# An attention stage of 32 samples written out in full in place of a loop on each engine

## What is computed

```python
x = x + 0.5 * ffn(layernorm(x))      # 2 of 8 experts per sample, chosen by its first row
x = x + attention(layernorm(x))      # 16 heads of 16, rotary positions, causal softmax
x = x + 0.5 * ffn(layernorm(x))

def attention(x):                    # b, t, d = 32, 512, 256
    q, k, v = split(x @ Wqkv.T)      # then heads; q and k are rotated
    scores = q @ k.T / 4, masked above the diagonal
    return merge(softmax(scores) @ v) @ Wo.T
```

## Time and profile before

| | |
|---|---|
| median of 3 runs | 2465.36 us (2464.51 to 2467.04) |
| the profiled execution | 2469.6 us |
| its span, first to last instruction | 2467.8 us |
| mean granted TensorE clock | 0.974 |
| TensorE (PE) busy | 2275.3 us, 92% of the span |
| VectorE (DVE) busy | 1969.7 us, 80% |
| ScalarE (ACT) busy | 1365.5 us, 55% |
| GpSimd (POOL) busy | 1275.4 us, 52% |

### The profile page before, as it was taken

How to read it: one execution, slowest core, us unless ns; L and a number is a source line. 1 busy time by engine, 2 the same in 40 slices (tenths; PEclk the granted TensorE clock), 3 DMA queues, 4 the chain that set the end, 5 groups by cost and what they waited for, 6 DMA issues and landing times. The chain is left out here.

```text
span 2467.8 us, 61020 instructions
## 1 busy us (share of the span) xinstructions
PE 2275.3 (92%) x18828; PEld 1422.1 (58%) x18828; DVE 1969.7 (80%) x4349; ACT 1365.5 (55%) x2567; POOL 1275.4 (52%) x1458
## 2 busy tenths in 40 slices
PE   2999999389999999999999999999999995999999
PEld 1666666146655555565555555655655552666666
DVE  4777776589889888898898898888988973777776
ACT  2455444046656666665566566656666663554454
POOL 2666665345445545554454455445544523666664
PEclk9999999589999999999999999999999997999999
DMA  4566665334543444344444444533443323566664
GB/s 159 167 210 202 196 195 181 78 61 95 97 88 87 88 88 87 88 92 84 88 87 92 83 88 92 98 82 81 95 94 88 79 53 103 188 198 195 206 207 163
DMA packets 281250, 296.35 MB, mean 120 GB/s; under 512 B 46096, under 2 KB 264048, under 8 KB 280944
## 3 DMA queue, kind: packets, MB, share of 16 engines
q1 hardware_dynamic: 280400, 291.34, 47.0%
q10 hardware_dynamic: 544, 1.05, 0.1%
HBM read 140.08 MB, written 83.89 MB: 91 GB/s over the span
## 5 line engine op out<-in xcount | busy, mean ns | idle before, releaser
L815 ACT ACTIVATE at_probs<-at_st_ps 128x512 f32<-128x512 f32 x1280 | 754.3, 603 | 553.6 <-PE at_st_ps L915 548.8
L745 DVE TENSOR_REDUCE at_mx<-at_mx_ps 128x1 f32<-128x512 f32 (+3 forms) x1408 | 842.4, 635 | 199.5 <-PE at_mx_ps L898 189.3
L667 POOL TENSOR_SCALAR_AFFINE_SELECT at_probs<-at_probs 128x512 f32<-128x512 f32 x512 | 318.7, 635 | 774.5 <-ACT at_probs L815 774.5
L896 PE MATMUL at_mx_ps<-at_k_stack,at_q_stack 128*128 128x512 f16 (+3 forms) x2048 | 539.8, 302 | 17.7 <-DMA at_k_stack<-qk_image 12.0
L915 PE MATMUL at_st_ps<-at_q_stack,at_k_stack 128*128 128x512 f16 (+3 forms) x2048 | 495.1, 303 | 43.1 <-issue 27.0
L898 PE MATMUL at_mx_ps<-mask,identb 128*128 128x128 bf16 x2048 | 387.0, 220 | 0.0
L420 ACT ACTIVATE f_h<-f_h_ps,f_b1s 128x512 f32<-128x512 f32 x256 | 175.9, 687 | 362.0 <-PE f_h_ps L462 351.0
L915 PEld LDWEIGHTS at_st_ps<-at_q_stack,at_k_stack 128*128 128x128 f16 x2048 | 167.6, 98 | 317.5 <-ACT at_probs L815 164.7
L932 PE MATMUL at_pv_ps<-at_probs,at_v 128*32 128x512 f32 (+3 forms) x4096 | 328.9, 439 | 1.2 <-POOL at_probs L667 0.6
L478 PE MATMUL f_y_ps<-f_w2hi,f_hhi 128*128 128x256 f16 x1024 | 279.3, 273 | 0.0
L478 PE MATMUL f_y_ps<-f_w2lo,f_hhi 128*128 128x256 f16 x1024 | 279.3, 273 | 0.0
(11 more groups left out here) (118 smaller groups left out, 3980.6 us busy)
## 6 DMA issues: line engine op xcount, KB each, us to landing
at_q_stack<-qk_image SPq DMA_DIRECT2D x192, 128.0 KB
at_k_stack<-qk_image SPq DMA_DIRECT2D x192, 128.0 KB, 4.4
f_x<-in_x SPq DMA_DIRECT2D x32, 512.0 KB, 5.7
f_w1hi<-w_hi SPq DMA_DIRECT2D x128, 128.0 KB, 2.5
f_w1lo<-w_lo SPq DMA_DIRECT2D x128, 128.0 KB, 2.2
f_b2s<-in_b SPq DMA_DIRECT2D x128, 128.0 KB, 3.8
f_w2hi<-w_hi SPq DMA_DIRECT2D x128, 128.0 KB, 4.2
f_w2lo<-w_lo SPq DMA_DIRECT2D x128, 128.0 KB, 4.2
```

The source lines that it names most:

```text
L667: nc.gpsimd.affine_select(out=ap, in_=ap, compare_op=ALU.is_ge, fill=0.0, base=0, pattern=[[0, d] for d in dims] + [[1, P]], channel_multi ...
L745: nc.vector.tensor_reduce(o_ap, i_ap, AX_X, ALU.max).then_inc(max_done, 1)
L815: nc.scalar.activation(probs[:, c, :], st_ps[c % 2][:], ACT.Exp, scale=DH ** -0.5).then_inc(exp_done, 1)
L896: nc.tensor.matmul(bank[:, at * w:at * w + w], q_stack[s.par][:, h, i * P:(i + 1) * P], k_stack[s.par][:, h // 2, 0:w], start=True, stop=F ...
```

## The change

`schedule` loses its hardware loop. One Python loop writes all samples from -1 to 32 out with `k = 0`. Each engine gets the same operations in the same order with the same waits; the values of the waits and the DRAM addresses of samples 3 to 28 become constants, as they were before and behind the loop. Buffers, semaphores and the other phases stay.

```diff
         def schedule(eng, slot):
             for g in (2, 3):
                 slot(At(0, -2), g)
-            for c in range(-1, 3):
-                for g in range(4):
-                    slot(At(0, c), g)
-            with eng.Fori(0, (B - 6) // 2) as k:
-                for c in (3, 4):
-                    for g in range(4):
-                        slot(At(k, c), g)
-            for c in range(B - 3, B + 1):
+            for c in range(-1, B + 1):
                 for g in range(4):
                     slot(At(0, c), g)
             slot(At(0, B + 1), 0)
```

## The result

The changed kernel takes 2428.05 us (median of 4 runs, 2427.58 to 2428.63) where the kernel before took 2464.94 us beside it: a ratio of 0.985, with a 95% interval of 0.9833 to 0.9867, or 36.9 us less. The forecast was 2429.3 us.

What follows compares the result with a forecast made beforehand. TensorE's pace bounds the attention phase, with 12 branches back stalling it. 23 us of stalls and 13 us of clock drops, 36.1 us by whole samples, off the 2465.4 us median give 2429.3 us; range 2419 to 2440 us.

Steps and rivals of the forecast that it cites:

- four branch-free samples: Steady-state attention samples without a branch back: 47.43, 47.52, 47.20 and 47.22 us, mean 47.34, taken as the straight code's pace.
- 46.99 behind a branch: Sample after a branch that left the clock alone, 46.99 us; used only for the range's end, a gain of 44.5 us.
- All alike: Sign of being right: attention samples of 47.0 to 47.5 us from store to store, all alike.
- a sign of being wrong: Samples over 47.6 us with no wait to show for it would make the four samples no fair measure.
- The two parts: Attention loop: 12 branches at 1.9 us, 23 us, plus seven pairs of samples slowed by clock drops, 13 us; together 36.
- rival 1: Clock still drops in attention, at some rate with dense work: gain only 23 us, time 2442.4 us; chance 0.07.
- Register work at nothing: Loop's register operations for waits and addresses, on all engines, are covered, so removing them gains nothing.
- More code at nothing: Writing out 26 samples instead of two costs nothing: the loop already loads its code again each iteration.
- The branch's price: TensorE's compare-and-branch at line 568: 3.42 us median as measured, against the skill's 108 ns, worth 1.3 us in all.
- covered by queued matmuls: Of each 3.42 us TensorE branch, 2.25 us leave the array idle; matmuls queued ahead cover the rest.
- Span and clock: Changed profile: span near 2431.7 us; granted clock 1.00 through attention, about 0.98 in the mean.

Runs made afterwards that it cites:

- pe_straight: Kernel before with only TensorE's code written out, the four other engines keeping the loop: 2427.06 us, ratio 0.9842.
- pe_loop: Kernel before with all engines written out except TensorE, which keeps the loop: 2476.72 us, ratio 1.0039.
- hint: Kernel before, loop kept, plus one TensorE instruction at the head of each iteration announcing the branch back: 2430.66 us, ratio 0.9848.
- stall_mid: Changed kernel plus 26 increments of an unused semaphore on TensorE at each of the 12 former branch places: 2477.14 us.
- hint_shift135: `hint` with 135 increments of an unused semaphore at the start of TensorE's code, moving its loop: 2481.44 us, late start included.
- four: Kernel before with four samples per loop iteration, 5 branches back instead of 12: 2448.93 us, ratio 0.9926.
- stall_short: Changed kernel plus 20 increments of an unused semaphore on TensorE at each of the 12 former branch places: 2446.41 us.

## Why the prediction was right

- **What bounds it.** TensorE's pace, and 12 branches of TensorE alone: `pe_straight` has the whole gain and `pe_loop` none of it. This is shown.
- **The sum.** 24 samples were forecast at 24 x 47.34 = 1136.2 us and took 1136.8, the gain 36.1 us and 35.5 in the trace, 36.9 between the medians. Taking the mean of the four branch-free samples, and not the 46.99 behind a branch, was right: in the changed kernel the common sample takes 47.27. That it hit within 0.6 us is luck all the same: the four spread by 0.3 us, which is 8 us in 24 samples, and the common sample alone would give 1134.5. "All alike" was not right, and three samples lie over 47.6 us, which I had named as a sign of being wrong. One of them (47.62) is not longer: TensorE did 434 matmuls in it and 427 in the next (46.92), where 430 is the rule, so the store that I cut at came late. The 47.60 and 47.59 are of that kind too. In the other two (47.79 and 48.12) the array waited 0.3 and 0.4 us for the transfer of `at_k_stack`, and a weight load 0.7 us. What makes that transfer late, and a few samples 0.1 to 0.3 us longer, is open.
- **The two parts.** Stalls 23 us, drops of the clock 13 us. The drops follow stalls, as the forecast had it, and rival 1 is out: no drop in the changed kernel's steady state, none in the loop of `hint`, 11 in `stall_mid`. The price of 1.9 us per drop also carries `pe_loop` and `stall_mid`. That a stall gives back a part of its idle time, 4 of 27 us, holds only where the other four engines loop too: `hint_shift135` and `four` give back 4 us in the same count, `pe_loop` and `stall_mid` 1 us. Some 2 us of it are no gift of the stall: `hint` and `pe_straight`, with loops on the other engines and no stall, take 1134.7 and 1134.8 us for the 24 samples, 2 us less than the changed kernel. The rest I can't explain.
- **Register work at nothing.** Right: `pe_straight` keeps it on four engines and `hint` on all five, and neither can be told from the changed kernel by its median.
- **More code at nothing.** Right in the sum, and the reason was sound as far as it went: q8 made 89 loads from 640 to 1860 us where the loop made 114. What I had not seen is why the loop loads at all. I took it as given that code is loaded anew each time; by the last runs it did so only because its body and the block behind it did not fit together.
- **The branch's price.** Reading 3.42 us off the row, against the 108 ns of the Trainium skill, decided the forecast. The reason that I quoted from the Trainium skill, a wait for code that is gone, was shown by `hint`: same branch, code present, 0.23 us. What I gave as covered by queued matmuls (3.42 less 2.25 us) was misread: at the first branch the array works for 1.7 us into the branch and starts again 0.4 us behind its end. The sum did not use it; the expectation for `stall_short` did.
- **Span and clock.** The clock came out at 0.983 for about 0.98. The span of 2426.8 us is 5 us under the 2431.7 that I gave. I had carried along the 4.2 us by which the first profiled execution lay above its median; the two traces differ by 6.5 us ahead of the first store, and I take those 4.2 us to be part of it.

## What to carry to other kernels

Look at the compare-and-branch rows of every engine: one that takes microseconds was waiting for code here, and the idle time of the array behind it, with the drops of the clock, is what leaving the loop can give back, here 3 us a branch. Writing out the one engine whose branch is long is enough; where code size matters, a hint on that engine's back edge does the same while the body fits its instruction memory. A loop near that size is fragile: instructions added far away, or taken out of it, moved this one by tens of microseconds without touching its work.

## What the runs showed of the hardware that was not expected

- The same taken branch of TensorE took 0.21 to 0.26 us with its target present, 2.8 to 3.9 us with one block to load, and 4.1 to 5.8 us with a second load under way.
- A hint of one instruction removed not one load per iteration but all nine.
- Idle stretches of 1.4 us brought no drop to the 1.2 GHz level at any of 12 places; stretches of 1.6 to 2.7 us brought it at 7 of 12 in two kernels (before, `hint_shift135`) and at 11 of 12 in two others (`pe_loop`, `stall_mid`), and in `four` one of 3.3 us brought none. In the kernel before, the length did not decide: a branch of 3.32 us (1116.4 us) had a drop behind it, and one of 3.69 us (1801.4 us) had none.
- Making the other four engines leaner cost 10 us (`pe_loop`), more than half of it through four more drops of TensorE's clock.
- Increments of a semaphore on TensorE are recorded with 51 ns and follow each other at 154 ns.
